# Second layer's mixture of experts: ways up as three products of 16-bit halves, computed two experts ahead

## The chip, the cores and the metric

One core of one Trainium2 chip. The metric is device time in microseconds (us) of one launch, the median of several runs. The core has a matmul engine (PE, with its weight loads PEld), a vector engine (DVE), an activation engine (ACT), GpSimd (POOL) and a queue engine (SP) that issues the DMAs. They run side by side and are ordered by semaphores only.

## The reference, cut to what matters

The model has four layers, each an attention over a context of 8 x 1500 rows followed by a feed-forward part, on 8 x 56 = 448 tokens of width 128. The change touches the feed-forward part of the second layer, a mixture of experts:

```
logits = x @ router_w.T                      # 16 experts, the best 2 of each token
w_full = sigmoid(top 2 logits), else 0
h      = silu(x @ gate_e) * (x @ up_e)       # each expert: 128 -> 128, twice
moe    = sum_e w_full[e] * (h @ down_e)
shared = silu(x @ sg) * (x @ su) @ sd        # width 256
x      = x + tanh(g_ffn[1]) * (moe + shared)
```

Here x is the normalised token matrix. All 16 experts are computed for all tokens and weighted afterwards; the shared part of width 256 is cut into two more "experts" of weight 1, which makes 18 in all.

## The kernel before, in words

The program is one hand-written instruction stream for each engine. The order within a stream is that of the code; between engines it is set by counting semaphores (`wait_ge` on one engine, `then_inc` on another).

The stage of the second layer's experts runs from about 322 to 367 us of the span. Names of its steps:

- The weights come in groups of three experts (`G1 = 3`, six groups). One DMA of 576 KB brings a group: for each expert 128 columns of gate, of up and of down, in 32-bit floats, into one of two buffers `wex[0]`, `wex[1]` (line 612). Groups 0 and 1 are loaded long before; group g + 2 is issued when group g's last product down is done (`ex_dn`).
- `gate_up1` (lines 1081 to 1088), called GU(e) from here on: PE computes gate and up of expert e, two products of 128x128 weights by 128x448 tokens, both operands 32-bit. Each such product shows as two MATMUL records in the trace, so GU(e) is four. Its two results go to PSUM banks 2, 3 or 4, 5 in turn.
- `silu1` (line 1564): ACT takes silu of the gate bank.
- `hidden1` (line 2332, recorded as line 1898 since all two-operand vector operations pass one helper): DVE multiplies it by the up bank; h goes to `xT2` or `xT3`.
- The product down (line 1099), called D(e): PE computes four products of 128x112 hidden values by 128x128 weights, both 32-bit, eight records in the trace, into bank 6 or 7.
- `weigh` (also recorded as line 1898): DVE multiplies the result of D(e) by the token's weight for e.
- `add_expert` (line 1798): POOL adds that to the running sum `y2`.

PE's order is GU(0), then for each e: GU(e + 1), D(e). GU(e + 1) waits for the hidden values of expert e - 1, whose banks it takes. D(e) waits for the hidden values of e and for the weighing of e - 2. DVE's order is hidden(e + 1), weigh(e). Both are written as hardware loops of two or six experts. Ahead of the loop DVE also works out the router's choice: two calls of `pick`, some 15 small instructions, between hidden(0) and weigh(0). ACT takes the router's sigmoid after silu(1).

Ahead of the stage stand the second layer's attention (lines 1010 to 1050 on PE; `probs1` and copies on ACT; `shift1` and `normalise1` on DVE), the output projection, the residual, a layer norm and four transposes, which give `xT`. Behind it DVE adds the sum and the last two experts' results to x (line 1942), and a layer norm leads on to the third layer's attention.

The fourth layer's experts (from about 753 us) already use three products of 16-bit halves: ACT rounds the 32-bit weights to 16 bits (`split_hi3`, line 1665: the high half), DVE subtracts that from the original (`split_lo3`, line 2548: the low half), the tokens are split alike, and PE sums high x high, high x low and low x high in one PSUM bank (line 1334).

Of the kernel before, what the change touches and what calls it, by code (L numbers as in the profile page):

```python
# [8 lines left out]
F16 = mybir.dt.float16  # L9
BF16 = mybir.dt.bfloat16  # L10
U8 = mybir.dt.uint8
ALU = mybir.AluOpType
# [101 lines left out]
SETS = 4  # L114
SQ = 6
G1 = 3

CTX_TOP, LATE_AT, SQK_AT = 19370, 23466, 29346

# [11 lines left out]

PRODUCT = {"latent_q": 14, "latent_k": 18, "latent_qT": 19, "queries2": 23, "queries3T": 36}

MAX_BANKS, TURN = (4, 5, 7), 24
MAX_AHEAD = 32
MAX_ORDER = [(0, u) for u in range(24)]
# [65 lines left out]
def build(nc, io, out):  # L202
    ctx = ExitStack()
    with ctx:
# [155 lines left out]
        w_r1 = carve([D, 16])  # L360
        sm16 = carve([TT, 8, NT, 16])
        wts = carve([TT, NT, E1])
        l1_end = at[0]
        ktmp = arena[:, ktmp_at:ktmp_at + B * D].rearrange("p (b n) -> p b n", b=B)
        at[0] = core_end
# [170 lines left out]
        def _(sp):  # L536
# [90 lines left out]
            for u in range(16, 24):  # L627
                if u == 19:
                    sp.wait_ge(rn_sq, 1)
                    for v in range(20, 24):  # L630
                        load_later(v)
                store_later(u)
                if u == 16:
                    sp.wait_ge(lv_full, 16 - IN_TURNS + 1)
                    load_experts1(0, 0)
                if u == 19:
                    sp.wait_ge(lv_full, 19 - IN_TURNS + 1)
                    load_experts1(1, 1)
# [5 lines left out]
            with sp.Fori(0, E1 // G1 // 2 - 1) as i:  # L644
                for p in range(2):
                    g = 2 * i + p
                    sp.wait_ge(ex_dn, G1 * (g + 1))
                    load_experts1(g + 2, p)


            sp.wait_ge(lat_ready, 1)
# [76 lines left out]
                load_gate_up3(e, e)  # L728
                load_down3(e, e)
            for e in range(E3 - 2):  # L730
                sp.wait_ge(ex_split, e + 1)
# [16 lines left out]
        def _(pe):  # L748
# [325 lines left out]
            op.next()  # L1074
            by_tokens(xT, w_r1, 1, cols=16)

            def w1(k, group, col):

                return wex[group][:, D * (3 * k + col):D * (3 * k + col) + D]

            def gate_up1(s, loads):

                if s % G1 == 0:
                    pe.wait_ge(ex_ld[s // G1 % 2], 16 * loads)
# [5 lines left out]
            def expert1(turn, s, more=True):  # L1090
                e = 2 * G1 * turn + s
                if more:

                    pe.wait_ge(ex_h, e + 1)
                    gate_up1(s + 1, turn + 1 + (s + 1) // (2 * G1))
                pe.wait_ge(ex_w, e + 1)
                pe.wait_ge(ex_h, e + 2)
                for t in range(NT):
                    mm = pe.matmul(ps[0:TT, 6 + s % 2, D * t:D * t + D],
                                   (xT2, xT3)[s % 2][:, TT * t:TT * t + TT], w1(s % G1, s // G1 % 2, 2),  # L1100
                                   start=True, stop=True)
                mm.then_inc(ex_dn, 1)

            gate_up1(0, 1)
            pe.wait_ge(lk_taken, 24 - IN_TURNS)
            pe.wait_ge(lv_taken, 24 - IN_TURNS)
            with pe.Fori(0, E1 // (2 * G1) - 1) as i:
                for s in range(2 * G1):
                    expert1(i, s)
            for s in range(2 * G1):  # L1110
                expert1(E1 // (2 * G1) - 1, s, more=s < 2 * G1 - 1)


            pe.wait_ge(ld_m, 5 * 16)
# [235 lines left out]
                mm.then_inc(ex_dn, 1)  # L1350

            def expert3(e, p):
                pe.wait_ge(ex_split, e + 1)
# [26 lines left out]
        def _(act):  # L1380
# [160 lines left out]
            later(20)  # L1541
            probs1(0)
            later(21)
            for i in range(NT):
                if i + 1 < NT:
# [12 lines left out]


            later(23)  # L1560

            def silu1(e, p):
                act.wait_ge(ex_gu, e + 1)
                act.activation(exs[p], ps[0:D, 2 + 2 * p, 0:N], ACT.Silu).then_inc(ex_act, 1)  # L1564

            silu1(0, 0)
            silu1(1, 1)
            act.wait_ge(to_act, 1)
            act.activation(sm16[:, 6], sm16[:, 0], ACT.Sigmoid).then_inc(from_act, 1)
            with act.Fori(1, E1 // 2) as i:  # L1570
                for p in range(2):
                    silu1(2 * i + p, p)


            act.wait_ge(l2_m, 1)
# [89 lines left out]
                act.copy(wh3[p][:, 0, :], wex[p][:, 0:2 * FF]).then_inc(ex_hi, 1)  # L1665

            def down_hi3(e, p):
                act.wait_ge(ex_ldd[p], 16 * (e // 2 + 1))
# [223 lines left out]
        def _(dve):  # L1892
# [4 lines left out]
            def tt(out, a, b, op):  # L1897
                return dve.tensor_tensor(out, a, b, op)  # L1898
# [397 lines left out]
            for i in range(NT):  # L2296
                if i + 2 < NT:
                    shift1(i + 2)
                if i == 2:

                    dve.wait_ge(rn_sd, 1)
                    ch.step(dve.reciprocal(rn_flat, rn_flat))
                normalise1(i)
            product_in.next()
            ch.link(tt(y, ps[0:TT, 0, :].rearrange("p (t n) -> p t n", t=NT), spread("L1_ob"), ALU.add))
            residual(1, y)
# [17 lines left out]
            layernorm(x, z, 1e-5)  # L2324
            signal(operand)
            turned(xT, 0)
            product_in.next()
            dve.tensor_copy(sm16[:, 0], ps[0:TT, 1, 0:64].rearrange("p (t n) -> p t n", t=NT)).then_inc(to_act, 1)

            def hidden1(e, p):  # L2330
                dve.wait_ge(ex_act, e + 1)
                tt((xT2, xT3)[p], ps[0:D, 3 + 2 * p, 0:N], exs[p], ALU.mult).then_inc(ex_h, 1)

            def weigh(e, p, weight, first):

# [11 lines left out]
                residual(k, big[:, :, D:2 * D])  # L2347
                dve.nop().then_inc(ex_acc, 1)

            hidden1(0, 0)  # L2350
            dve.wait_ge(to_act, 1)
            pick(sm16, 16, 0, NEG)
            hidden1(1, 1)
# [6 lines left out]
            weigh(0, 0, wts[:, :, 0:1], 0)  # L2360
            hidden1(2, 0)
            weigh(1, 1, wts[:, :, 1:2], 0)
            with dve.Fori(1, E1 // 2 - 1) as i:
                for p in range(2):
                    e = 2 * i + p
                    hidden1(e + 1, 1 - p)
                    weigh(e, p, wts[:, :, bass.ds(e, 1)], 0)
            hidden1(E1 - 1, 1)
            dve.wait_ge(ex_acc, E1)
            residual(5, y2)  # L2370
            for e in range(E1 - 2, E1):
# [172 lines left out]

            def split_lo3(e, p):

                dve.wait_ge(ex_hi, e + 1)
# [144 lines left out]
```

## Time and profile before

| what | value |
|---|---|
| median of 3 runs | 826.67 us (825.04 to 827.05) |
| the profiled execution's own time | 825.94 us |
| its span | 824.1 us |
| PE busy | 735.4 us (89%) |
| DVE busy | 615.2 us (75%) |
| ACT busy | 438.3 us (53%) |
| POOL busy | 347.0 us (42%) |
| mean granted TensorE clock | 0.943 of full |

The span is measured from the first to the last instruction; 1.8 us of the profiled execution's time lie around it. Busy shares are averages over stages with different limits, so the stage of the change has to be read by itself.

### The profile page before, as it was taken

The page shows a single profiled execution, that of the slowest core. Times are in us where ns is not written, and L with a number is a line of the kernel's source. Part 1 is how long each engine was busy: PE and PEld are TensorE (multiplying, and loading weights), DVE is VectorE, ACT ScalarE, POOL GpSimd, SP SyncE. Part 2 cuts the span into 40 slices and gives each one's busy share as a digit, 9 for nine tenths or more (in the row PEclk, how much of TensorE's full clock was granted, in tenths as well). Part 3 has the DMA queues.
Part 4 walks back from the last instruction along what each step waited for, and adds up shares of the span by engine and source line. Part 5 has one row for each costly group of instructions (what it writes and reads, how often), then busy time and mean ns, then how long its engine had stood idle before and what let it go on. Part 6 is the DMA issues. An engine that isn't in the chain of part 4 may idle for free.

```text
span 824.1 us, 15426 instructions
## 1 busy us (share of the span) xinstructions
PE 735.4 (89%) x5468; PEld 469.1 (57%) x5468; DVE 615.2 (75%) x1297; ACT 438.3 (53%) x739; POOL 347.0 (42%) x283
## 2 busy tenths in 40 slices
PE   3799999997886978998899999998899999898997
PEld 3577787776544465663455555563346666653443
DVE  4779999998878765567565566658689999516786
ACT  2656667677484433435444545432127776743674
POOL 0665555561523501640677787740242211102464
PEclk8999999999998878999999999999859999999999
DMA  8267767532424512206022333007736678101520
GB/s 208 75 205 252 252 198 227 173 117 72 98 67 131 160 51 76 86 29 177 3 79 78 104 100 101 6 10 103 128 71 131 124 126 165 37 2 64 180 78 12
DMA packets 50645, 89.71 MB, mean 109 GB/s; under 512 B 17427, under 2 KB 34779, under 8 KB 50099
## 3 DMA queue, kind: packets, MB, share of 16 engines
q1 hardware_dynamic: 50578, 88.83, 39.8%
q8 instruction: 42, 0.69, 0.4%
q14 instruction: 25, 0.20, 0.1%
HBM read 63.29 MB, written 25.52 MB: 108 GB/s over the span
## 4 chain that ended last, share of the span: by engine, by line
PE 29%; DVE 17%; POOL 2%; ACT 2%; issue 2%; DVEq 0%; POOLq 0%; ACTq 0%
DVE arena L2516 11%; PE ps L1165 9%; PE ps L1155 7%; PE ps L1334 3%; PE ps L1348 2%; DVE arena L1898 2%; POOL arena L1820 2%; PE ps L1270 2%; PE ps L1259 1%; ACT arena L1647 1%; PE ps L1201 1%; PE ps L1242 1%; PE ps L1313 1%; PE ps L1171 1%; PE ps L768 1%
## 5 line engine op out<-in xcount | busy, mean ns | idle before, releaser
L2516 DVE TENSOR_REDUCE arena<-ps 112x1 f32<-112x500 f32 x192 | 114.6, 670 | 9.0 <-PE ps L1242 9.0
L1820 POOL TENSOR_TENSOR arena<-arena 125x448 f32<-125x448 f32 x96 | 109.2, 1137 | 24.6 <-ACT arena L1606 20.7
L1898 DVE TENSOR_TENSOR arena<-ps,arena 128x448 f32<-128x448 f32 (+7 forms) x139 | 80.8, 612 | 37.5 <-ACT arena L1564 18.3
L1647 ACT ACTIVATE arena<-ps 125x896 f32<-125x896 f32 x96 | 87.2, 917 | 23.5 <-PE ps L1259 23.4
L1165 PE MATMUL ps<-arena 125*128 125x448 f32 (+1 forms) x208 | 97.2, 548 | 2.0 <-ACT arena L1606 1.5
L1606 ACT ACTIVATE arena<-arena,kbias 125x448 f32<-125x448 f32 x96 | 63.6, 668 | 65.4 <-DVE arena L1898 47.9
L1898 DVE TENSOR_TENSOR arena<-ps,rn 125x448 f32<-125x448 f32 x96 | 59.2, 618 | 47.0 <-PE ps L1155 42.1
L843 PE MATMUL ps<-w_k2h,arena 128*125 128x512 f16 x288 | 69.4, 392 | 11.6 <-ACT arena L1416 10.4
L1155 PE MATMUL ps<-arena 128*125 128x448 f16 (+3 forms) x312 | 76.5, 354 | 1.2 <-DVEq L1909 1.1
L1155 PEld LDWEIGHTS ps<-arena 128*125 128x125 f16 (+1 forms) x312 | 40.1, 133 | 54.8 <-issue 41.8
L1416 ACT ACTIVATE arena<-ps 125x512 f32<-125x512 f32 x96 | 55.4, 598 | 12.4 <-PE ps L843 9.8
L843 PEld LDWEIGHTS ps<-w_k2h,arena 128*125 128x125 f16 x288 | 39.2, 140 | 36.5 <-ACT arena L1416 14.5
L2052 DVE TENSOR_REDUCE rn<-arena 125x8 f32<-125x512 f32 x96 | 59.0, 679 | 0.8 <-ACT arena L1416 0.8
L1242 PE MATMUL ps<-arena 64*112 64x500 f16 x192 | 55.4, 444 | 2.5 <-issue 1.2
L1732 POOL TENSOR_TENSOR arena<-arena 128x500 f16<-128x500 f32 x24 | 27.4, 1144 | 69.4 <-ACT arena L1403 69.2
L1270 PE MATMUL ps<-arena 125*32 125x168 f32 x768 | 48.6, 325 | 2.3 <-ACT arena L1647 1.8
L1898 DVE TENSOR_TENSOR arena<-arena 125x12 f32<-125x12 f32 (+6 forms) x79 | 45.9, 597 | 6.2 <-ACT arena L1681 4.7
L866 PE MATMUL ps<-w_l,arena 128*125 128x256 f32 x192 | 44.7, 390 | 1.8 <-ACT arena L1443 1.8
L1165 PEld LDWEIGHTS ps<-arena 125*128 125x128 f32 (+1 forms) x208 | 37.7, 189 | 14.6 <-issue 8.8
L1334 PE MATMUL ps<-arena 128*128 128x448 f16 x192 | 40.9, 361 | 5.5 <-DVE arena L1898 5.5
L1716 POOL TENSOR_TENSOR arena<-arena 112x4 f32<-112x4 f32 x9 | 9.2, 1027 | 83.6 <-DVE arena L1922 75.1
L1259 PE MATMUL ps<-arena 64*125 64x112 f16 x768 | 43.5, 235 | 0.0
(323 smaller groups left out, 1462.7 us busy)
## 6 DMA issues: line engine op xcount, KB each, us to landing
arena<-in_ctxT SPq DMA_DIRECT2D x8, 750.0 KB, 9.3
d_cln<-arena SPq DMA_DIRECT2D x8, 750.0 KB
d_clnT<-arena SPq DMA_DIRECT2D x8, 750.0 KB
d_k<-arena SPq DMA_DIRECT2D x24, 250.0 KB
d_v<-arena SPq DMA_DIRECT2D x24, 250.0 KB
arena<-d_clnT SPq DMA_DIRECT2D x8, 750.0 KB
arena<-in_ctx SPq DMA_DIRECT2D x8, 672.0 KB
arena<-d_cln SPq DMA_DIRECT2D x8, 672.0 KB
```

Source lines behind the costliest of these rows:

```text
L843: mm = pe.matmul(ps[0:KP, k, :], clnT[p][:, a, KP * j:KP * j + KP], w_k2h[:, w, :], start=(n == 0), stop=(n == 2))
L1155: mm = pe.matmul(ps[0:rows, (t + p) % 2, 0:N].rearrange("p (h q) -> p h q", h=H8), clnT_s[p][:, a, cols:cols + rows], qtT[:, q, :, bass.ds ...
L1165: pe.matmul(ps[0:D, 4 + 2 * p, 0:N], cln_s[p][0:rows, t, :], pexp[(t + p) % 2][0:rows], start=(t == 0), stop=(t == KT)).then_inc(l2_pv, 1)
L1242: pe.matmul(ps[0:TT, max_bank(bn, u), 0:500], q.rearrange("p o h q -> p (o h q)"), kst[bn % 3][64 * r:64 * r + 64, g, 500 * third:500 * th ...
L1270: pe.matmul(ps[32 * g:32 * g + 32, 6, 0:168], v3s[p][:, t, 32 * g:32 * g + 32], p3[t % 2][:, 3 * g:3 * g + 3, :].rearrange("p h q -> p (h ...
L1334: mm = pe.matmul(ps[0:D, 2 + 2 * (c % 2) + m, 0:N], wh3[p][:, w, at:at + D], xTh[:, a, :], start=(n == 0), stop=(n == 2))
L1606: act.activation(pexp[(t + p) % 2][0:rows], sscl[(t + p) % 2][0:rows], ACT.Exp, bias=bias)\
L1647: act.activation(p3[t % 2].rearrange("p (k h) q -> p k (h q)", k=2), ps[0:KP, 2 * (t % 2):2 * (t % 2) + 2, 0:8 * S], ACT.Exp).then_inc(l3_ ...
L1820: ins = pool.tensor_tensor(psum2[p][0:rows], psum2[p][0:rows], pexp[(t + p) % 2][0:rows], ALU.add)
L1898: return dve.tensor_tensor(out, a, b, op)
L2052: dve.tensor_reduce(rn[:, bass.ds(turn - 1, 1), j, :].rearrange("p o h -> p (o h)"), sqk[:, j % SQ, :].rearrange("p (h d) -> p h d", h=H8) ...
L2516: dve.tensor_reduce(mx3[bn % 2][:, u % 2, u % 8 // 2, u // 8:u // 8 + 1], ps[0:TT, max_bank_of(bn, u), 0:500], AX.X, ALU.max).then_inc(l3_ ...
```

## The change

- GU(e) becomes six 16-bit products in place of two 32-bit ones: high x high, high weights x low tokens, low weights x high tokens, for gate and for up. Banks come in three pairs, (2, 3), (4, 5), (0, 1), and the hidden values and silu results in three buffers.
- PE's order becomes GU(0), GU(1), then for each e: GU(e + 2), D(e). GU(e) waits for the halves of its group (`ex_split`) and for hidden(e - 3).
- New on ACT: `split_hi1(g)`, the rounding of a group's 768 columns of gate and up; groups 0 and 1 in the attention, ahead of `probs1(3)`; groups 2 to 5 after silu(3), silu(6), silu(9) and silu(12). Also the rounding of `xT`.
- New on DVE: `split_lo1(g)`, the subtraction; groups 0 and 1 after the last `normalise1`, groups 2 to 5 after hidden(3), hidden(6), hidden(9) and hidden(12). Also the low half of `xT`, between the copy that makes `xT` and the copy of the router's logits.
- DVE's order becomes weigh(e), hidden(e + 2).
- The group's load is two DMAs: gate and up (384 KB), issued as soon as the halves of the group before it in the same buffer are made; down (192 KB), issued after that group's last D. The halves and third buffers lie in `kblk`, which the attention has left.
- The loops are written out. The fourth layer's waits on the shared counters are moved by what is counted here.

```diff
-            def load_experts1(g, p):
-                sp.dma_start(wex[p][:, 0:G1 * 3 * D], batch(io["L1_ex"], g)).then_inc(ex_ld[p], 16)
+            def load_gate_up1(g, p):
+                sp.dma_start(wex[p][:, 0:GU1], io["L1_ex"][g, :, 0:GU1]).then_inc(ex_ld[p], 16)
+            def load_down1(g, p):
+                sp.dma_start(wex[p][:, GU1:G1 * 3 * D], io["L1_ex"][g, :, GU1:G1 * 3 * D]).then_inc(ex_ldd[p], 16)
...
+            sp.wait_ge(ex_split, 2)
+            for p in range(2):
+                load_gate_up1(2 + p, p)
+            for g in range(E1 // G1 - 2):
+                sp.wait_ge(ex_dn, G1 * (g + 1))
+                load_down1(g + 2, g % 2)
+                if g + 4 < E1 // G1:
+                    sp.wait_ge(ex_split, g + 4)
+                    load_gate_up1(g + 4, g % 2)
...
+            def gate_up1(e):
+                g, at = e // G1, e % G1 * 2 * D
+                pe.wait_ge(ex_split, 3 if g < 2 else g + 2)
+                if e > 2:
+                    pe.wait_ge(ex_h, e - 1)
                 for m in range(2):
-                    mm = pe.matmul(ps[0:D, 2 + 2 * (s % 2) + m, 0:N], w1(s % G1, s // G1 % 2, m), xT,
-                                   start=True, stop=True)
+                    for n, (w, a) in enumerate(((0, 0), (0, 1), (1, 0))):
+                        mm = pe.matmul(ps[0:D, UP_BANKS1[e % 3] - 1 + m, 0:N], wh1[g % 2][:, w, at + D * m:at + D * m + D],
+                                       x1h[:, a, :], start=(n == 0), stop=(n == 2))
...
+            gate_up1(0)
             pe.wait_ge(lk_taken, 24 - IN_TURNS)
             pe.wait_ge(lv_taken, 24 - IN_TURNS)
+            gate_up1(1)
+            pe.wait_ge(to_act, 1)
+            for e in range(E1):
+                if e + 2 < E1:
+                    gate_up1(e + 2)
+                down1(e)
...
+            def split_hi1(g):
+                act.wait_ge(ex_ld[g % 2], 16 * (g // 2 + 1))
+                if g > 1:
+                    act.wait_ge(ex_gu, G1 * (g - 1))
+                act.copy(wh1[g % 2][:, 0, :], wex[g % 2][:, 0:GU1]).then_inc(ex_hi, 1)
...
+            act.wait_ge(operand, OPERAND["latentsT"] - 2)
+            act.copy(x1h[:, 0, :], xT).then_inc(ex_hi, 1)
...
+            def split_lo1(g):
+                dve.wait_ge(ex_hi, g + 1 if g < 2 else g + 2)
+                tt(wh1[g % 2][:, 1, :], wex[g % 2][:, 0:GU1], wh1[g % 2][:, 0, :], ALU.subtract).then_inc(ex_split, 1)
...
+            for e in range(E1 - 2):
+                weigh(e, e % 2, wts[:, :, e:e + 1], 0)
+                hidden1(e + 2)
+                if e % G1 == 1 and e // G1 + 2 < E1 // G1:
+                    split_lo1(e // G1 + 2)
```

## Rows read from the trace of the kernel before

**Rows 1.** Busy time by stretch, the stage: from:to us, length, engines, clock, DMA.
```profile
322.00:366.30 44.30, 43.58 (x218) 29.14 (x217) 24.98 (x51) 21.60 (x28) 20.28 (x16) 1.00 0.22 75
```

**Rows 2.** Timeline of the stage: start us, us, engine, line, operation, [idle before <- releaser].
```profile
359.66 1.28 ACT L1564 ACT_TABLE_LOAD   x1
359.77 1.67 PE L1086 MATMUL ps<-arena,wex 128*128 128x448 f32 x4
361.04 1.27 POOL L1798 TENSOR_TENSOR arena<-arena 112x512 f32<-112x512 f32 x1 [1.11 <-DVE arena L1898]
361.27 1.04 PE L1099 MATMUL ps<-wex,arena 128*112 128x128 f32 x8
...
362.05 1.22 DVE L1898 TENSOR_TENSOR arena<-ps,arena 128x448 f32<-128x448 f32 x2 [1.16 <-ACT arena L1564]
362.15 1.67 PE L1086 MATMUL ps<-arena,wex 128*128 128x448 f32 x4
```

**Rows 3.** The chain that ended last: start us, us, what.
```profile
398.20 0.75 PE ps L1165 x2
398.96 0.57 PE ps L1155 x3
...
789.80 2.27 PE ps L1348 x12
```

**Rows 4.** Timeline of the stage's start.
```profile
321.99 3.25 PE L1086 MATMUL ps<-arena,wex 128*128 128x448 f32 x8
...
323.78 0.54 ACT L1564 ACTIVATE arena<-ps 128x448 f32<-128x448 f32 x1 [4.88 <-PE ps L1086]
...
328.98 2.35 DVE L1898 TENSOR_TENSOR arena<-ps,arena 112x512 f32<-112x512 f32 x4
...
330.25 1.13 PE L1099 MATMUL ps<-wex,arena 128*112 128x128 f32 x8 [0.21 <-DVE arena L1898]
...
331.53 0.69 DVE L1898 TENSOR_TENSOR arena<-ps,arena 112x512 f32<-112x512 f32 x1 [0.20 <-PE ps L1099]
```

**Rows 5.** Timeline of the fourth layer's experts, which work with halves.
```profile
752.11 1.22 DVE L1898 TENSOR_TENSOR arena<-wex,arena 128x1024 f16<-128x1024 f32 x1
...
753.46 2.43 PE L1334 MATMUL ps<-arena 128*128 128x448 f16 x12
...
754.79 0.54 ACT L1675 ACTIVATE arena<-ps 128x448 f32<-128x448 f32 x1 [0.31 <-PE ps L1334]
755.24 1.04 ACT L1665 CAST arena<-wex 128x1024 f16<-128x1024 f32 x1
...
761.23 0.56 ACT L1681 CAST arena<-arena 128x448 f16<-128x448 f32 x1 [2.38 <-DVE arena L1898]
...
761.83 0.63 DVE L1898 TENSOR_TENSOR arena<-arena 128x448 f16<-128x448 f32 x1 [0.63 <-ACT arena L1681]
...
777.60 1.34 DVE L1898 TENSOR_TENSOR arena<-arena 128x448 f16<-128x448 f32 x1 [0.69 <-ACT arena L1681]
```

**Rows 6.** Timeline of the second layer's attention and what follows it.
```profile
298.04 1.06 ACT L1539 ACTIVATE arena<-arena 128x1024 f32<-128x1024 f32 x1 [3.93 <-DVE arena L1898]
...
313.65 0.69 DVE L1898 TENSOR_TENSOR arena<-ps,vec 112x512 f32<-112x512 f32 x1 [2.96 <-PE ps L760]
```

**Rows 7.** Timeline of the DMA queue, and the landing of line 612's loads.
```profile
320.26 0.52 SPq L642 DMA_DIRECT2D arena<-in_L_wq  x1
...
DMA to landing us min/median/max: 3.5/3.7/7.8
```

**Rows 8.** Timeline of the stage's end.
```profile
366.75 0.75 DVE L1942 SCALAR_TENSOR_TENSOR x<-ps,tg,x 112x512 f32<-112x512 f32 x1 [0.25 <-DVE x L1942]
```

**Rows 9.** Busy time by stretch, around the stage (columns as in rows 1).
```profile
300.00:310.00 10.00, 7.97 (x37) 7.41 (x35) 5.63 (x7) 1.57 (x4) 0.00 (x0) 0.50 0.01 2
368.00:372.00 4.00, 4.00 (x24) 2.07 (x21) 3.52 (x17) 1.02 (x1) 1.06 (x1) 0.57 0.00 0
384.00:388.00 4.00, 2.98 (x8) 1.52 (x10) 2.27 (x5) 1.20 (x3) 0.00 (x0) 0.64 1.06 268
```

More of the change, by code:

```diff
@@ L116 @@
 G1 = 3
+GU1 = G1 * 2 * 128
+SPLITS1 = 7
 CTX_TOP, LATE_AT, SQK_AT = 19370, 23466, 29346
@@ L132 @@
 PRODUCT = {"latent_q": 14, "latent_k": 18, "latent_qT": 19, "queries2": 23, "queries3T": 36}
+UP_BANKS1 = (3, 5, 1)
 MAX_BANKS, TURN = (4, 5, 7), 24
@@ L362, in build @@
         wts = carve([TT, NT, E1])
+        wh1, h1, ex1 = [], [xT2, xT3], [exs[0], exs[1]]
+        for p in range(2):
+            words = kblk[p].rearrange("p e h s -> p (e h s)")
+            wh1.append(words[:, 0:768].bitcast(F16).rearrange("p (w n) -> p w n", w=2))
+            (h1, ex1)[p].append(words[:, 768:768 + N])
+        x1h = kblk[0].rearrange("p e h s -> p (e h s)")[:, 768 + N:768 + 2 * N].bitcast(F16).rearrange("p (w n) -> p w n", w=2)
         l1_end = at[0]
@@ L634, in _ @@
                     sp.wait_ge(lv_full, 16 - IN_TURNS + 1)
-                    load_experts1(0, 0)
+                    load_gate_up1(0, 0)
+                    load_down1(0, 0)
                 if u == 19:
                     sp.wait_ge(lv_full, 19 - IN_TURNS + 1)
-                    load_experts1(1, 1)
+                    load_gate_up1(1, 1)
+                    load_down1(1, 1)
             sp.wait_ge(lv_full, 23 - IN_TURNS + 1)
@@ L642, in _ @@
                 sp.dma_start(dst, io[name]).then_inc(ld_m, 16)
[L644 to L648, printed above, removed]
+            sp.wait_ge(ex_split, 2)
+            for p in range(2):
+                load_gate_up1(2 + p, p)
[5 more added lines that the diff above has]
+                    load_gate_up1(g + 4, g % 2)
             sp.wait_ge(lat_ready, 1)
@@ L730, in _ @@
             for e in range(E3 - 2):
-                sp.wait_ge(ex_split, e + 1)
+                sp.wait_ge(ex_split, SPLITS1 + e + 1)
                 load_gate_up3(e + 2, e % 2)
@@ L1075, in _ @@
             by_tokens(xT, w_r1, 1, cols=16)
[L1077 to L1084, printed above, removed]
+            def gate_up1(e):
[3 more added lines that the diff above has]
+                    pe.wait_ge(ex_h, e - 1)
@@ L1085, in gate_up1, with down1 @@
                 for m in range(2):
-                    mm = pe.matmul(ps[0:D, 2 + 2 * (s % 2) + m, 0:N], w1(s % G1, s // G1 % 2, m), xT,
-                                   start=True, stop=True)
+                    for n, (w, a) in enumerate(((0, 0), (0, 1), (1, 0))):
+                        mm = pe.matmul(ps[0:D, UP_BANKS1[e % 3] - 1 + m, 0:N], wh1[g % 2][:, w, at + D * m:at + D * m + D],
+                                       x1h[:, a, :], start=(n == 0), stop=(n == 2))
                 mm.then_inc(ex_gu, 1)
[L1090 to L1095, printed above, removed]
+            def down1(e):
+                g = e // G1
+                if e % G1 == 0:
+                    pe.wait_ge(ex_ldd[g % 2], 16 * (g // 2 + 1))
@@ L1096, in expert1 @@
                 pe.wait_ge(ex_w, e + 1)
                 pe.wait_ge(ex_h, e + 2)
+                at = GU1 + e % G1 * D
                 for t in range(NT):
-                    mm = pe.matmul(ps[0:TT, 6 + s % 2, D * t:D * t + D],
-                                   (xT2, xT3)[s % 2][:, TT * t:TT * t + TT], w1(s % G1, s // G1 % 2, 2),
-                                   start=True, stop=True)
+                    mm = pe.matmul(ps[0:TT, 6 + e % 2, D * t:D * t + D], h1[e % 3][:, TT * t:TT * t + TT],
+                                   wex[g % 2][:, at:at + D], start=True, stop=True)
@@ L1102, in expert1 @@
                 mm.then_inc(ex_dn, 1)
-            gate_up1(0, 1)
+            gate_up1(0)
             pe.wait_ge(lk_taken, 24 - IN_TURNS)
             pe.wait_ge(lv_taken, 24 - IN_TURNS)
[L1107 to L1111, printed above, removed]
+            gate_up1(1)
[4 more added lines that the diff above has]
+                down1(e)
@@ L1352, in expert3 @@
             def expert3(e, p):
-                pe.wait_ge(ex_split, e + 1)
+                pe.wait_ge(ex_split, SPLITS1 + e + 1)
                 for c in range(4):
@@ L1543, in _ @@
             later(21)
+            def split_hi1(g):
[3 more added lines that the diff above has]
+                act.copy(wh1[g % 2][:, 0, :], wex[g % 2][:, 0:GU1]).then_inc(ex_hi, 1)
             for i in range(NT):
+                if i == NT - 2:
+                    act.wait_ge(l1_s, NT)
+                    split_hi1(0)
+                    split_hi1(1)
                 if i + 1 < NT:
@@ L1560, in _, with silu1 @@
             later(23)
-            def silu1(e, p):
+            act.wait_ge(operand, OPERAND["latentsT"] - 2)
+            act.copy(x1h[:, 0, :], xT).then_inc(ex_hi, 1)
+            def silu1(e):
                 act.wait_ge(ex_gu, e + 1)
[L1564 to L1572, printed above, removed]
+                act.activation(ex1[e % 3], ps[0:D, UP_BANKS1[e % 3] - 1, 0:N], ACT.Silu).then_inc(ex_act, 1)
+            for e in range(E1):
+                silu1(e)
+                if e == 1:
+                    act.wait_ge(to_act, 1)
+                    act.activation(sm16[:, 6], sm16[:, 0], ACT.Sigmoid).then_inc(from_act, 1)
+                if e % G1 == 0 and 1 < e // G1 + 1 < E1 // G1:
+                    split_hi1(e // G1 + 1)
             act.wait_ge(l2_m, 1)
@@ L2303, in _ @@
                 normalise1(i)
+            def split_lo1(g):
+                dve.wait_ge(ex_hi, g + 1 if g < 2 else g + 2)
+                tt(wh1[g % 2][:, 1, :], wex[g % 2][:, 0:GU1], wh1[g % 2][:, 0, :], ALU.subtract).then_inc(ex_split, 1)
+            split_lo1(0)
+            split_lo1(1)
             product_in.next()
@@ L2326, in _, with hidden1 @@
             turned(xT, 0)
+            dve.wait_ge(ex_hi, 3)
+            dve.wait_ge(operand, OPERAND["latentsT"] - 2)
+            tt(x1h[:, 1, :], xT, x1h[:, 0, :], ALU.subtract).then_inc(ex_split, 1)
             product_in.next()
             dve.tensor_copy(sm16[:, 0], ps[0:TT, 1, 0:64].rearrange("p (t n) -> p t n", t=NT)).then_inc(to_act, 1)
-            def hidden1(e, p):
+            def hidden1(e):
                 dve.wait_ge(ex_act, e + 1)
-                tt((xT2, xT3)[p], ps[0:D, 3 + 2 * p, 0:N], exs[p], ALU.mult).then_inc(ex_h, 1)
+                tt(h1[e % 3], ps[0:D, UP_BANKS1[e % 3], 0:N], ex1[e % 3], ALU.mult).then_inc(ex_h, 1)
             def weigh(e, p, weight, first):
@@ L2348, in weigh_last @@
                 dve.nop().then_inc(ex_acc, 1)
-            hidden1(0, 0)
+            hidden1(0)
             dve.wait_ge(to_act, 1)
             pick(sm16, 16, 0, NEG)
-            hidden1(1, 1)
+            hidden1(1)
             pick(sm16, 16, 1, NEG)
@@ L2358, in _ @@
             ch.link(dve.memset(wts[:, :, 16:E1], 1.0))
[L2360 to L2368, printed above, removed]
+            for e in range(E1 - 2):
[3 more added lines that the diff above has]
+                    split_lo1(e // G1 + 2)
             dve.wait_ge(ex_acc, E1)
@@ L2639 @@
                                a["L1_ffn_shared_down_w"][:, D * k:D * k + D].T], axis=1) for k in range(2)]
+    all1 = np.concatenate([experts1, np.stack(shared1)]).reshape(-1, G1, D, 3 * D)
     io = {
```

8 lines of the change are left out of this document (4 added, 4 removed).

## The prediction

> **What bounds the kernel now.** I read the page first, but its shares are averages over stages, so next the view of busy time by stretch for the stage of the second layer's experts. [...] PE bounds the stage. The timeline gives its period: GU(16) starts at 359.77, D(15) at 361.27, GU(17) at 362.15 [rows 2]. So GU takes a slot of 1.50 us, D one of 0.88, an expert 2.38. The other engines wait inside it: DVE sat idle 1.16 us for the silu, POOL 1.11 us for DVE [rows 2]. Behind the stage the token path goes on without a branch (residual, layer norm, projections, the third attention), so what the stage's end gains, the whole gains.
>
> **PE's slots.** GU goes from two 32-bit products to six 16-bit ones of the same 448 columns. The fourth layer has such products back to back: 12 in 2.27 us, 0.189 each [rows 3]. Six make 1.135 in place of 1.50. D keeps its 32 bits and its 0.88. Does a change of type between them cost something? In the third layer three 16-bit products and one 32-bit product alternate, 398.20 + 0.75 = 398.95 and the next begins at 398.96 [rows 3]; nothing. New period 1.135 + 0.88 = 2.02 us, 0.365 less. [...] I take 0.365, from back-to-back work.
>
> **Does the chain of hand-overs fit into 2.02?** D(e)'s start to weigh(e)'s start is 331.53 - 330.25 = 1.28 us [rows 4]. DVE's pair of weigh and hidden takes 1.22 [rows 2], the hand-over to PE about 0.15 (an estimate: the four vector operations end at 328.98 + 2.35 = 331.33, of which the second, hidden(2), at about 330.15; D(2) starts at 330.25 [rows 4]). So D(e) to D(e + 2) needs 1.28 + 1.22 + 0.15 = 2.65, and has 4.04. On the other side GU's start to silu takes 754.79 - 753.46 = 1.33 [rows 5], so GU(e + 2)'s silu is done 1.33 + 0.54 = 1.87 after its start, and D(e + 2) follows 5.2 us after it. Looking two experts ahead leaves both loops slack of over a microsecond. PE stays the bound.
>
> **DVE's new work in the stage.** The low half of 768 columns lies between 448 columns at 0.63 and 1024 at 1.22 [rows 5], 0.95 in proportion. Three experts cost 3 x 1.22 + 0.95 = 4.6 of 6.05 us. One instruction can be stretched: the subtraction at 777.60 took 1.34 in place of 0.63 with GpSimd at work beside it [rows 5], 0.7 more. With it DVE has 5.3 of 6.05; still covered. If the cover were gone (over 1.4 us more for each of the four halves), the excess would be paid four times.
>
> [...]
>
> **ACT.** A silu is 0.54; four roundings of 768 columns lie between 0.56 and 1.04 [rows 5], 0.8 each. ACT has 3 x 0.54 + 0.8 = 2.4 of 6.05 us. The loops reload a table before every other silu, 1.28 us, which lies in ACT's wait for PE [rows 2]; the unrolled form drops seven of nine or so. That was hidden, so it earns nothing.
>
> **The start.** Halves of groups 0 and 1: ACT's 2 x 0.8 go ahead of probs1(3), where ACT waited 3.93 us for DVE [rows 6]; DVE's 2 x 0.95 go into the 2.96 us that it waited for the projection [rows 6]. Their loads were issued by 278 and land within 7.8 [rows 7]. Cost nothing; if that cover failed, up to 1.6 + 1.9. The token halves lie on the path: after `xT` ACT rounds (0.56), DVE subtracts (0.63) [rows 5], and then PE may begin; the router's eight products fill part of it, and GU(0) starts about 322.45 in place of 321.99. But what ends last is DVE's chain: silu(0), hidden(0), the router's small instructions, weigh(0), hidden(2), then D(2) at 330.25, where PE had waited [rows 4]. silu(0) comes 1.33 after GU's start with 16 bits and came 323.78 - 321.99 = 1.79 after it [rows 4], so silu(0) moves from 323.78 to 323.8. D(2) stays at 330.25 to 330.4: I take +0.1. The gain of the first experts' shorter GU thus goes into PE's wait there. Bounds: 0 to +0.5.
>
> **From D(2) on.** After D(2) come 13 periods to D(15) in both orders (a GU and a D each): 13 x 0.365 = 4.75. In the trace D(15) starts at 361.27, and (361.27 - 330.25) / 13 = 2.386, so no stall hides in between.
>
> **The tail.** D(15), weigh(15), POOL's add, three residuals. GU(17) no longer stands between D(15) and D(16), but the third residual does not wait for them: it runs right behind the second (idle 0.25) [rows 8], and all three behind POOL. Before, DVE did hidden(16) between D(15) and weigh(15), late by 0.05; now weigh comes at once. D(17) waits for hidden(17), behind weigh(15): 1.28 + 1.22 + 0.15 = 2.65 after D(15), and its result is there before the third residual. D(15)'s start to the end stays 367.50 - 361.27 = 6.2. Change 0, bounds -0.1 and +0.3.
>
> **Loads.** Twelve DMAs for six; four more issues of some 0.5 us [rows 7] beside an idle SP. Gate and up of groups 2 and 3 are now issued right behind the third layer's weights (320.26 and on [rows 7]); even at the longest landing of 7.8 [rows 7] they are there by 329.6, and split_hi1(2) is due at about 329.8, its halves at 334. Down of group g + 2 has three D's of time, 6 us, against 3.7. SP's two new waits stand ahead of nothing but these loads until the latents' store, 5 us after the stage. Counters of the fourth layer are only renumbered.
>
> **Sum.** 4.75 - 0.1 = 4.6 us. The profiled execution took 825.94, so 821.3; it lies 0.7 below the median of 826.67, against which later medians are to be held: 822.1.
>
> **The rivals.**
> 1. The period doesn't fall to 2.02, because hand-overs and waits on PE's queue (two or three before each group of products) leave gaps. For it: PEld shows idle "issue" gaps everywhere. Against: they lie under running products. At 0.15 a period more, 2 us of the gain go: 824.1; at the full 0.365 nothing is left: 826.7. I give 0.10, around 824.6.
> 2. More than forecast: DVE's chain at the start ends earlier, since ACT and PE are less in its way, and D(2) comes up to 1 us sooner, or a dip of the clock behind the stage goes away. In 384 to 388 us the granted clock was 0.64, in 368 to 372 it was 0.57 [rows 9], with keep-up products and critical ones in them. 820.0; 0.08.
> 3. [...] 823.6; 0.06.
> 4. Slower than before: the clock falls in the stage. PE now has a wait before GU(0) and one before D(2); from 300 to 310 us, where it was busy 8.0 of 10 us, the grant was 0.50 [rows 9]. [...] Against it: PE is 98% busy in the stage of before [rows 1], both new waits are under half a microsecond, and the fourth layer's halves run at 0.189 each, the full clock, in a stage with waits too [rows 3]. 0.05.
>
> The rest, 0.71, is the forecast with its own range of 820.6 to 823.6.
>
> **How the numbers follow.** Likeliest 822.0. 820.2 to 824.6 takes in the slot's bounds (1.21: 1.0 later), the start's, the clock both ways and part of the first rival. What this measurement can tell from no change is about 0.3%, 2.5 us: faster is below 824.2, slower above 829.1. Faster: 0.71 + 0.08 + 0.06 and a little of the first rival, 0.86; same 0.09; slower 0.05.
>
> **What would show it.** In the changed trace GU as six records with the next D 1.14 behind it; a period of 2.02 from D(2) to D(15); D(2) at 330.3; DVE idle in each period, split_lo1 at 0.95 to 1.7; the third residual's end at 362.9 in place of 367.5; the same distance from there to the end. A period above 2.1, a D(2) after 331, a clock below 1.00 in the stage, or a part behind the stage that grew would make it wrong.

## The result, and the profile after

The changed kernel takes 822.12 us (median of 20 runs, 816.84 to 829.01) beside 827.14 us for the kernel before (20 runs, 822.48 to 830.12): ratio 0.9952, 95% interval 0.9931 to 0.9973. In absolute terms that is 4.0 us less by the ratio (2.2 to 5.7) and 5.0 by the medians. Forecast were 822.0 us and 4.6 less. That the median lies within 0.1 us of the forecast is luck: runs of one kernel spread over more than 1%, and the parts below miss by more. So the parts of the forecast are read from the profiles, where the same stretch repeats to a few hundredths of a microsecond.

Three marks cut the kernel into parts: the start of DVE's copy that makes the transposed tokens (from there the stage is measured, its length called T), the end of the third residual, and the first product of the third layer's attention. From the page of the changed kernel:

```profile
span 818.4 us, 15421 instructions
```

| part, us | before | changed | difference |
|---|---|---|---|
| up to the transposed tokens | 320.50 | 322.08 | +1.58 |
| T, the stage | 47.00 | 41.66 | -5.34 |
| of it: tokens to D(2) | 9.75 | 9.68 | -0.07 |
| of it: D(2) to D(15), 13 periods | 31.02 | 26.22 | -4.80 |
| of it: D(15) to the third residual's end | 6.23 | 5.76 | -0.47 |
| from there to the third layer's first product | 25.35 | 24.17 | -1.18 |
| the rest of the span | 431.25 | 430.49 | -0.76 |
| span | 824.1 | 818.4 | -5.7 |

The stage was profiled a second time in both kernels: T 47.00 again before, 41.65 changed. The first and the last part vary from profile to profile of any kernel here (317.0 to 322.1 and 430.5 to 436.2). So the change's own effect is the 5.35 of the stage; the first profiles' 5.7 holds other things that nearly cancel. The part behind the stage repeated in each kernel (25.35 and 25.34 before, 24.17 twice in the changed one). Its busy rows (from:to us, length, PE, PEld, DVE, ACT, POOL, granted clock, DMA share, GB/s), before and changed, show where the difference comes from, a mean granted clock of 0.87 and 1.00:

```profile
367.50:392.85 25.35, 21.42 (x85) 10.10 (x85) 20.01 (x48) 11.77 (x22) 1.06 (x1) 0.87 0.56 145
363.74:387.91 24.17, 18.20 (x84) 8.52 (x85) 19.91 (x48) 11.52 (x22) 1.06 (x1) 1.00 0.59 152
```

The 1.58 us more ahead of the tokens do not come from the new halves of groups 0 and 1. These lie wholly in waits. First the kernel before, then the changed one:

```profile
311.57 2.05 PE L760 MATMUL ps<-arena 128*112 128x128 f32 x8 [0.34 <-ACT arena L1532]
```
```profile
299.08 1.06 ACT L1555 ACTIVATE arena<-arena 128x1024 f32<-128x1024 f32 x1 [2.46 <-DVE arena L1926]
...
312.30 1.83 DVE L1926 TENSOR_TENSOR arena<-wex,arena 128x768 f16<-128x768 f32 x2
313.15 2.05 PE L778 MATMUL ps<-arena 128*112 128x128 f32 x8 [0.34 <-ACT arena L1548]
...
315.23 0.69 DVE L1926 TENSOR_TENSOR arena<-ps,vec 112x512 f32<-112x512 f32 x1 [1.10 <-PE ps L778]
```

ACT's wait fell from 3.93 us to 2.46 and DVE's from 2.96 to 1.10 ([rows 6] has both of before), and from the projection's first product to the tokens it is 320.50 - 311.57 = 8.93 before and 322.08 - 313.15 = 8.93 after.

Busy time over the whole of T, in the same columns, first the kernel before between the same two marks, since [rows 1] covers a shorter stretch, then the changed one. PE's waits now lie at the two ends, and DVE's share has risen by the new halves, from 57% to 78%:

```profile
320.50:367.50 47.00, 45.02 (x227) 30.05 (x225) 26.56 (x53) 21.60 (x28) 20.28 (x16) 1.00 0.23 77
322.08:363.74 41.66, 38.41 (x263) 28.17 (x261) 32.61 (x58) 17.25 (x27) 21.21 (x16) 1.00 0.27 86
```

The timeline of one period with a split (start us, us, engine, line, operation, idle before), beside [rows 2]. GU is now six records of 16 bits; GU(10) starts at 342.75, D(8) at 343.89, 1.14 later, and the next GU at 344.76; 344.76 - 342.75 is the period, 2.01:

```profile
342.52 0.82 ACT L1564 CAST arena<-wex 128x768 f16<-128x768 f32 x1
...
342.75 1.30 PE L1103 MATMUL ps<-arena 128*128 128x448 f16 x6
342.95 1.22 DVE L1926 TENSOR_TENSOR arena<-ps,arena 112x512 f32<-112x512 f32 x2 [0.79 <-PE ps L1115]
...
343.79 1.27 POOL L1826 TENSOR_TENSOR arena<-arena 112x512 f32<-112x512 f32 x1 [0.58 <-DVE arena L1926]
343.89 1.03 PE L1115 MATMUL ps<-wex,arena 128*112 128x128 f32 x8
...
344.09 1.78 DVE L1926 TENSOR_TENSOR arena<-wex,arena 128x768 f16<-128x768 f32 x1
...
344.76 1.30 PE L1103 MATMUL ps<-arena 128*128 128x448 f16 x6
```

The subtraction took 1.78 us: POOL's add had begun at 343.79 and ended at 345.06, and the subtraction ended at 345.87, 0.81 later. In all four groups: 0.95, 1.78, 1.78, 1.78. In the first it was the add that took longer, 2.14 in place of 1.27 (332.61 to 334.75), although its record starts 0.05 before the subtraction's.

The stage's start, beside [rows 4]: D(2) at 331.76 is 9.68 us behind the tokens; weigh(0) starts at 330.39, hidden(2) follows it, and PE still waits for that:

```profile
322.08 0.62 DVE L1976 COPY arena<-ps 128x448 f32<-128x448 f32 x1 [0.79 <-PE ps L772]
...
322.74 0.56 ACT L1588 CAST arena<-arena 128x448 f16<-128x448 f32 x1 [3.63 <-DVE arena L1976]
...
324.02 3.59 PE L1103 MATMUL ps<-arena 128*128 128x448 f16 x18 [0.30 <-DVE arena L1926]
325.37 0.55 ACT L1592 ACTIVATE arena<-ps 128x448 f32<-128x448 f32 x1 [0.76 <-PE ps L1103]
...
330.39 2.35 DVE L1926 TENSOR_TENSOR arena<-ps,arena 112x512 f32<-112x512 f32 x4
...
331.73 0.93 PEld L1115 LDWEIGHTS ps<-wex,arena 128*112 128x112 f32 x8 [0.54 <-issue]
331.76 1.10 PE L1115 MATMUL ps<-wex,arena 128*112 128x128 f32 x8
```

The stage's end, beside [rows 8]. DVE waits 0.91 for POOL's last add, and the three residuals follow:

```profile
357.98 1.91 PE L1115 MATMUL ps<-wex,arena 128*112 128x128 f32 x16
...
359.05 1.22 DVE L1926 TENSOR_TENSOR arena<-ps,arena 112x512 f32<-112x512 f32 x2 [0.79 <-PE ps L1115]
359.88 1.26 POOL L1826 TENSOR_TENSOR arena<-arena 112x512 f32<-112x512 f32 x1 [0.74 <-DVE arena L1926]
...
361.19 0.75 DVE L1970 SCALAR_TENSOR_TENSOR x<-arena,tg,x 112x512 f32<-112x512 f32 x1 [0.91 <-POOL arena L1826]
361.97 0.75 DVE L1970 SCALAR_TENSOR_TENSOR x<-ps,tg,x 112x512 f32<-112x512 f32 x1
362.99 0.75 DVE L1970 SCALAR_TENSOR_TENSOR x<-ps,tg,x 112x512 f32<-112x512 f32 x1 [0.26 <-DVE x L1970]
```

### The profile page after: what moved, and what is told of

Same layout as the page of the kernel before. It is cut to its first block, busy times and chain, and to the rows that moved or that the text cites. A ratio compares the mean times of both kernels' runs of the same rounds, so it can differ in the third digit from the quotient of the medians.

```text
span 818.4 us, 15421 instructions
## 1 busy us (share of the span) xinstructions
PE 727.2 (89%) x5504; PEld 467.2 (57%) x5504; DVE 623.2 (76%) x1304; ACT 434.1 (53%) x739; POOL 348.1 (43%) x283
## 4 chain that ended last, share of the span: by engine, by line
PE 30%; DVE 16%; ACT 3%; POOL 2%; issue 2%; DVEq 0%; POOLq 0%; ACTq 0%
DVE arena L2550 10%; PE ps L1181 9%; PE ps L1171 6%; PE ps L1350 3%; PE ps L1286 2%; PE ps L1364 2%; DVE arena L1926 2%; PE ps L1275 2%; POOL arena L1848 2%; PE ps L1258 1%; ACT arena L1675 1%; PE ps L1217 1%; PE ps L1329 1%; PE ps L1187 1%; PE ps L786 1%
## 5 line engine op out<-in xcount | busy, mean ns | idle before, releaser
L1926 DVE TENSOR_TENSOR arena<-arena 125x12 f32<-125x12 f32 (+7 forms) x80 | 46.5, 598 | 6.8 <-ACT arena L1709 4.7
L1874 POOL COPY arena<-arena 4x448 f16<-4x448 f16 x16 | 8.9, 554 | 80.4 <-ACT arena L1661 79.9
```

## The experiments

Parts of T in every profile, in us. A dip is a stretch, 3.4 us long or twice that, in which the granted clock is at its lower level, 0.50 of the full one (337.93 to 341.34 of the version with one load, for example); the last column says whether one lay at the stage's start.

| kernel | tokens to D(2) | 13 periods | tail | T | behind the stage | clock's dip at the start |
|---|---|---|---|---|---|---|
| before, two profiles | 9.75 | 31.02 | 6.23 | 47.00 | 25.35, 25.34 | no |
| changed, two profiles | 9.68, 9.67 | 26.22 | 5.76 | 41.66, 41.65 | 24.17 | no |
| 32-bit products, order of the change, two | 12.53 | 30.93 | 5.76 | 49.22 | 25.39, 25.40 | yes |
| one ahead, 16 bits | 9.67 | 26.22 | 6.00 | 41.89 | 24.17 | no |
| two products | 9.30 | 21.30 | 5.76 | 36.36 | 25.39 | no |
| two products, no low halves | 9.29 | 21.30 | 5.76 | 36.35 | 25.28 | no |
| subtractions twice | 9.67 | 28.73 | 5.76 | 44.16 | 25.21 | no |
| one load for a group | 10.91 | 48.89 | 5.76 | 65.56 | 24.97 | yes |
| other tail | 11.06 | 26.15 | 4.87 | 42.08 | 25.32 | yes |
| other tail, PE kept busy | 9.68 | 26.22 | 4.87 | 40.77 | 25.67 | no |
| one choice of the router | 10.95 | 26.15 | 5.76 | 42.86 | 25.80 | yes |

**32-bit products in the change's order.** Everything of the change but the halves:

```diff
-                    for n, (w, a) in enumerate(((0, 0), (0, 1), (1, 0))):
-                        mm = pe.matmul(..., wh1[g % 2][:, w, at + D * m:at + D * m + D],
-                                       x1h[:, a, :], start=(n == 0), stop=(n == 2))
+                    mm = pe.matmul(..., wex[g % 2][:, at + D * m:at + D * m + D], xT, start=True, stop=True)
...
+                sp.wait_ge(ex_gu, G1 * (g + 1))
+                load_gate_up1(g + 2, g % 2)
```

> The changed kernel's order (two experts ahead), three bank pairs, three buffers, written-out loops, and loads of ways up and down apart, but products of 32-bit operands and no halves at all. Stage T = from the start of the copy that makes the transposed tokens to the end of the third residual; 47.0 us in the kernel before, 41.7 in the changed one. Theory A (PE's slots set the period; only the shorter products pay): period 2.38 to 2.39 us from D(2) to D(15), T 46.3 to 47.0 (only the tail, where weigh(15) no longer stands behind hidden(16), gives 0.3 to 0.5), whole kernel within 1 us of before. Rival B (the order, the loads apart or the written-out loops carry a good part): period under 2.25, T below 45, whole kernel 2 us or more faster than before.

The period stayed at 30.93 / 13 = 2.38 us and the tail gave its 0.47: theory A, for these two parts. T was 49.22, outside both theories, and the whole kernel slower than before, ratio 1.0033 (1.0007 to 1.0058). The loss stands at the start, where D(2) came 2.8 us later: three GUs took 6.45 us.

> The kernel with 32-bit products, two ahead, once more. Its first profile had T 49.2, of which 2.8 were a dip of the clock at the start, and its time was 3 us over before. Theory: the dip comes and goes, so T is 46.4 in a profile without it, 49.2 with it, and the period 2.38 in both. Rival: this order always has the dip or another cost, T 49.2 again.

It was 49.22 again (ratio 1.0023, 1.0000 to 1.0045). The rows of the second profile, first PE's timeline, then the granted clock:

```profile
322.57 6.45 PE L1099 MATMUL ps<-arena,wex 128*128 128x448 f32 x12
328.86 1.04 PE L1111 MATMUL ps<-wex,arena 128*112 128x128 f32 x8
...
332.12 1.67 PE L1099 MATMUL ps<-arena,wex 128*128 128x448 f32 x4
333.62 1.04 PE L1111 MATMUL ps<-wex,arena 128*112 128x128 f32 x8
```
```profile
322.00:326.00 4.00, 4.00 (x13) 2.20 (x13) 0.23 (x1) 0.32 (x1) 0.00 (x0) 0.61 0.66 232
```

Twelve records at the full clock are 12 x 0.375 = 4.5 us; here D(0) starts 328.86 - 322.57 = 6.29 us after GU(0), since for 3.4 us the clock was at its lower level, where a record took 0.75 us in place of 0.375. So the dip is 1.8 of the 2.8 us; the expectation above, and below that of the version with PE kept busy, put all 2.8 down to it, which is wrong. The other 1.0 is the order's own: ahead of D(2) PE now has five GUs and two D's in place of four and two. From the tokens that is 1.48 + 5 x 1.50 + 2 x 0.88 = 10.74 us even without a dip, where DVE's chain needed 9.75 before. With 16-bit GUs the same five fit under the chain (9.68). Without the dip T would be about 47.4 (an estimate, 49.22 - 1.8), not 46.4. The rival "a dip or another cost" stands: two profiles of two show 49.22, and the whole times agree (1.8 + 1.0 - 0.6 for periods and tail = 2.2 us or 0.27%).

**One expert ahead.**

```diff
-                if e + 2 < E1:
-                    gate_up1(e + 2)
+                if e + 1 < E1:
+                    gate_up1(e + 1)
                 down1(e)
```

> The changed kernel with its 16-bit products, but only one expert ahead as before: PE GU(e+1), D(e); DVE hidden(e+1), weigh(e); the low half of a group made after weigh(2), weigh(5), weigh(8), weigh(11). Theory A (slots set the period; a hand-over GU to D takes 2.67 us and has 3.15): period 2.02 to 2.1, at most some 0.2 us lost at each of the four split places, T 41.9 to 43.0. Rival B (the look-ahead carries the gain): T 45 to 47.

T 41.89, at the lower end of theory A, with the full 26.22 of the changed kernel. Looking two experts ahead buys nothing for the period; all that is lost is 0.24 of the tail, since hidden(16) stands ahead of weigh(15) again. Time 823.85 us, ratio 0.9969 (0.9944 to 0.9995). Two rows show what the later place of the split does:

```profile
343.31 0.95 DVE L1925 TENSOR_TENSOR arena<-wex,arena 128x768 f16<-128x768 f32 x1
...
343.54 1.85 POOL L1825 TENSOR_TENSOR arena<-arena 112x512 f32<-112x512 f32 x1 [0.74 <-DVE arena L1925]
```

Here DVE began first, took its 0.95, and POOL's add was the one that stretched, to 1.85.

**Two products.** `enumerate(((0, 0), (0, 1)))` in place of the three; then also without the subtraction:

```diff
+                if g < 2:
                     tt(wh1[g % 2][:, 1, :], wex[g % 2][:, 0:GU1], wh1[g % 2][:, 0, :], ALU.subtract).then_inc(ex_split, 1)
+                else:
+                    dve.nop().then_inc(ex_split, 1)
```

> The changed kernel without the third product of each way up (low weights by high tokens left out), halves made as before. PE's slots shrink from 2.02 to 1.64 us. Theory A alone: period 1.64, T 36.8. Theory C (DVE is the next bound, because the four subtractions were stretched to 1.78 us beside GpSimd: 3 x 1.22 + 1.78 = 5.4 us for three experts): period 1.80 to 1.85 over the groups with a split, T 38.5 to 39.5.

> As the one with two products (the third left out), and DVE's low halves of groups 2 to 5 left out too (a nop signals in their place). Theories A and C: DVE and GpSimd have 1.22 and 1.27 us of 1.64, so period 1.64 to 1.66, T 36.6 to 37.2. If hand-overs bound instead (D(e) to D(e+2) 2.5 us against 3.28), period above 1.7.

Both periods are 21.30 / 13 = 1.64 us: PE's slots again, and theory C fell. T is 36.36 and 36.35, a little under what was expected, since D(2) came sooner too. The subtractions took 0.95 in all four groups with two products: three began within 0.06 us of the start of POOL's add, the second 0.12 before the end of one (333.09, the add's end at 333.21), and POOL's adds beside them took 1.9 to 2.1. I had carried 1.78 over to another rhythm. The first two of them:

```profile
328.42 0.95 DVE L1926 TENSOR_TENSOR arena<-wex,arena 128x768 f16<-128x768 f32 x1
333.09 0.95 DVE L1926 TENSOR_TENSOR arena<-wex,arena 128x768 f16<-128x768 f32 x1
```

One more reading: D(2) came 0.37 us sooner, as GU(0) is 0.38 shorter, though PE's work ahead of D(2) shrank by 5 x 0.38 = 1.9. So a chain from silu(0) over DVE sets D(2), not PE's sum.

**Each subtraction twice.**

```diff
+                if g > 1:
+                    ch.link(tt(wh1[g % 2][:, 1, :], wex[g % 2][:, 0:GU1], wh1[g % 2][:, 0, :], ALU.subtract))
```

> The changed kernel with each of DVE's four subtractions in the stage made twice over. Theory A with C (DVE covered, but only just: 3 x 1.22 + 1.78 = 5.4 of 6.05 us): now about 6.4 of 6.05, so PE waits some 0.3 to 0.6 us for each group, T 42.3 to 43.8. If the halves were on the path already, each copy would cost its whole 0.95 to 1.8: T 45.5 to 48. If DVE had ample room: T 41.7.

T 44.16, a little over the range: 2.5 us more, of which 1.05 in the first group and 0.49 in each of the other three. A group now takes 6.53 us (341.61 to 348.13 below), set by DVE: two subtractions 2.97 and three pairs.

```profile
341.61 2.97 DVE L1926 TENSOR_TENSOR arena<-wex,arena 128x768 f16<-128x768 f32 x2
344.50 2.34 DVE L1926 TENSOR_TENSOR arena<-ps,arena 112x512 f32<-112x512 f32 x4
346.99 1.22 DVE L1926 TENSOR_TENSOR arena<-ps,arena 112x512 f32<-112x512 f32 x2 [0.15 <-PE ps L1115]
```

So the halves are covered in the changed kernel: in those three groups DVE had 1.2 us more, of which 0.5 reached the end and 0.7 was room; in the first it had 1.9 more (2.89 for 0.95), of which 0.9 was room.

**One load for a group**, as before, after its last D:

```diff
-                load_down1(g + 2, g % 2)
-                if g + 4 < E1 // G1:
-                    sp.wait_ge(ex_split, g + 4)
-                    load_gate_up1(g + 4, g % 2)
+                load_group1(g + 2, g % 2)
```

> The changed kernel with one DMA of 576 KB for a group of three experts, issued after the group's last product down, as in the kernel before; all else as changed. Theory: ACT's rounding of group g stands behind silu(3g-3) and then waits for a load issued only after D(3g-4), 3.7 us long, and the silu behind it waits with it; some 2.8 us for each of four groups, T 50 to 54, slower than before by 3 to 7 us. Rival (the separate loads are of no consequence, since the old load had time enough): T 41.7.

Time 846.48 us, ratio 1.0222 (1.0172 to 1.0273); T 65.56, far over my 50 to 54. The direction was right and the size less than half: 24 us more than the changed kernel, where 8 to 12 were expected. The timeline shows the ring (PE, ACT and SP):

```profile
331.18 11.86 SPq L621 DMA_DIRECT2D wex<-in_L_ex  x2
...
334.80 0.83 ACT L1561 CAST arena<-wex 128x768 f16<-128x768 f32 x1 [5.24 <-DMA wex<-in_L_ex]
...
336.68 1.31 PE L1100 MATMUL ps<-arena 128*128 128x448 f16 x6 [3.51 <-DVE arena L1923]
...
339.69 2.12 PE L1100 MATMUL ps<-arena 128*128 128x448 f16 x6
...
346.77 0.83 ACT L1561 CAST arena<-wex 128x768 f16<-128x768 f32 x1 [8.20 <-DMA wex<-in_L_ex]
```

A group took 346.77 - 334.80 = 11.97 us in place of 6.05. The load of a group waits for three D's that come only after the silus queued behind the rounding of the group ahead, so load, rounding, silu and three experts follow one another instead of overlapping; and behind a wait of PE of 3.5 us the granted clock was at 0.50 from 337.93 to 341.34 (2.12 us for six products). The change's loads "apart" are what makes halves possible at this place of ACT's queue; another place for the rounding was not tried.

**Other tail.** Expert 16's residual ahead of the wait for POOL:

```diff
-            dve.wait_ge(ex_acc, E1)
-            residual(5, y2)
             for e in range(E1 - 2, E1):
+                if e == E1 - 1:
+                    dve.wait_ge(ex_acc, E1)
+                    residual(5, y2)
```

> The changed kernel as it is, on the same chip as the one with the other tail. T 41.5 to 41.8, whole kernel 0.4 to 0.7% under before. The part from the stage's end to the third layer's first product was 24.2 us in its first profile and 25.4 before; theory: that is the clock's dips, so it varies from run to run between about 24 and 25.5 whatever the kernel.

T was 41.65 as expected, the time 0.59% under before. The part behind the stage was 24.17 once more, so its theory, that this part varies from run to run whatever the kernel, is not borne out: all three kernels with two profiles repeated their own value (the last is 25.39 and 25.40 of the 32-bit version).

> The changed kernel with the three last residuals in another order: expert 16's result is added to x while GpSimd still makes the last sum, then the sum, then expert 17. Theory A: the tail from D(15) to the last residual is a chain weigh(15), GpSimd's add 1.27, three residuals of 0.75; one residual moves into DVE's wait of 0.91 for GpSimd, T 40.7 to 41.0, whole kernel 0.8 us less than the changed one (too little for its time to show). Rival: expert 16's result is late and the order gains nothing, T 41.6.

The tail fell from 5.76 to 4.87 as worked out, DVE's wait for POOL from 0.91 to 0.26:

```profile
356.41 0.74 DVE L1970 SCALAR_TENSOR_TENSOR x<-ps,tg,x 112x512 f32<-112x512 f32 x1
357.40 0.75 DVE L1970 SCALAR_TENSOR_TENSOR x<-arena,tg,x 112x512 f32<-112x512 f32 x1 [0.26 <-POOL arena L1826]
358.31 0.75 DVE L1970 SCALAR_TENSOR_TENSOR x<-ps,tg,x 112x512 f32<-112x512 f32 x1 [0.15 <-DVE x L1970]
```

T itself was 42.08, since this profile had the dip at the start (+1.39). Of the complete versions this has the lowest median: 820.67 us, ratio to before 0.9911 (0.9883 to 0.9939), beside 822.10 and 0.9941 (0.9913 to 0.9970) of the changed kernel on the same chip. The intervals overlap; that it beats the kernel before is shown, that it beats the changed one only by the profile's 0.89.

**PE kept busy around the stage.** The other tail, and more keep-up products (`keep_clock`: products that nobody reads, run while PE would wait): 11 in place of 6 ahead of the token transposes, 10 new ones behind D(17), 11 in place of 7 ahead of the latents' transposes.

> The changed kernel with the tail's new order and more keep-up products on TensorE where it waits around the stage: 11 in place of 6 ahead of the token transposes, 10 new ones behind D(17), 11 in place of 7 ahead of the latents' transposes. In the profiles so far the clock was at its lower level for about 3.5 us either right behind the start of the stage (T + 1.4 with 16-bit products, + 2.8 with 32-bit ones) or at two places behind it (25.3 in place of 24.2 us from the stage's end to the third layer's first product). Theory F (the dips follow the waits just ahead of them, where PE was busy 0.65 of 2 us): start and end of the stage stay at 1.00, T 40.7 to 40.9, the part behind 24.2 to 24.8 (the dip before the query products isn't filled), whole kernel 0.6 to 1.0% under before. Rival (the dips come whatever PE does there): one of them in this profile too.

No dip at the start nor right behind the stage, T 40.77, as theory F said. The changed kernel's two profiles have none at either place without the filling, so this one profile doesn't show that the filling kept them away. And ahead of the third layer the clock was low for 6.8 us and soon after for another 3.4, and the part behind rose to 25.67; time 823.19, ratio 0.9958 (0.9935 to 0.9981), no better than the changed kernel:

```profile
320.00:325.00 5.00, 4.80 (x29) 2.99 (x30) 2.91 (x12) 3.59 (x6) 0.00 (x0) 1.00 0.82 303
359.03:363.00 3.97, 3.97 (x30) 2.16 (x29) 3.29 (x17) 1.01 (x1) 1.06 (x1) 1.00 0.00 0
376.00:380.00 4.00, 3.44 (x10) 1.82 (x12) 2.24 (x5) 1.25 (x4) 0.00 (x0) 0.50 1.07 260
```

**One choice of the router** (`pick(sm16, 16, 1, NEG)` left out, a product of the first choice with itself in its place, so the second expert of each token is missing from the result).

> The changed kernel with the router's second choice left out (a single small product in its place, so some 1.5 us less in DVE's chain ahead of weigh(0)). Theory (DVE's chain sets D(2), PE waits 0.3 to 0.5 us for it): D(2) 9.3 to 9.4 us after the transposed tokens in place of 9.67, no more, because PE's own slots set it then; T 41.3. Rival (D(2) was set by PE or by the halves): 9.67, T 41.65.

Inconclusive: this profile had the dip, and D(2) at 10.95 says no more than the 11.06 and 10.91 of the two other 16-bit versions with one. The two products above speak for DVE's chain instead.

**The kernel before, a second profile.**

> The kernel before as it is, a second profile. Its first had no dip of the clock at the stage's start (T 47.0) and two behind it (25.4 to the third layer's first product). The kernel with 32-bit products two ahead had the dip at the start in both of its profiles. [...]

T 47.00 and 25.34 behind: no dip at the start and two behind the stage, as in the first profile. Why this kernel has none at the start and the 32-bit version of the new order has one each time, it doesn't tell.

## Why the prediction was right

- PE bounds, and the period falls from 2.38 to 2.02: measured 26.22 / 13 = 2.017. Shown by taking it apart: 32-bit products in the new order keep 2.38, 16-bit ones in the old order reach 2.02, two products give 1.64. Rival 1 (gaps in the hand-overs) is out. The 13 periods gave 4.80 for 4.75. The stage as a whole gave 5.34 where the sum had 4.65: 0.05 more from the periods, 0.17 from the start and 0.47 from the tail. The 1.21 us for a GU in the forecast's range is half the 2.43 of [rows 5]; no run shows such a slot: six records took 1.14 (342.75 to D(8) at 343.89); only their modelled end is at 1.30.
- D(2) stays where it was: 9.75 became 9.68, forecast +0.1. silu(0) came 1.35 us after GU(0)'s start, as [rows 5] had it at 1.33. The halves of groups 0 and 1 cost nothing, as forecast: 8.93 us from the projection to the tokens in both kernels.
- The tail was the term mis-sized: forecast 0 (bounds -0.1 and +0.3), measured -0.47, beyond its bounds. I had seen that hidden(16) no longer stands ahead of weigh(15) but took 1.28 from D to weigh from [rows 4]; that row is not of the steady rhythm: its D had waited 0.21 for DVE, its weights were loaded only then, and its record is 1.13 long where the steady ones are 1.03. In the steady rhythm it is 342.95 - 341.88 = 1.07. The same step missed that hidden(17) stood ahead of the first residual before: POOL's add ended at 364.69 and DVE was free for the residual at 364.97.
- Splits: ACT 0.82 each, DVE 0.95 to 1.78 (forecast 0.95 to 1.7), all covered, as doubling them showed. Where POOL had begun first, by 0.3 us, the subtraction ended 0.81 us after POOL's add, and with DVE first it was POOL that took longer (1.85 for 1.27). The 0.83 more lie near my 0.7 from [rows 5], and DVE had room for them: 3 x 1.22 + 1.78 = 5.4 of 6.05 us.
- Loads: in time; gate and up took 3.5 to 7.8 us to land, down 2.3 to 7.6, so none more than the forecast's longest, and no rounding in the stage waited for one. What I did not weigh was what they would cost if not apart: 24 us.
- The clock: rival 2 spoke of the dips of [rows 9]. In both profiles of the changed kernel they were gone (24.17 for 25.35), which is rival 2's condition, yet the time did not come out at its 820.0. Of the variants, all but the one that looks one ahead show at least one of them. So 1.2 us of the first profile's gain come from the clock and not from the stage. They repeated in the second pair of profiles, but the whole time leaves little room for them: 5.35 + 1.2 = 6.5 lies above its interval of 2.2 to 5.7. No run here ties them to the edit.

Open: why the dip at the start came in both profiles with 32-bit products two ahead, in neither of the kernel before, and in some with 16 bits.

## What to carry to other kernels

Where TensorE's slots bound a loop, write down the slot of each product from back-to-back records at hand, and the longest hand-over beside it; if the hand-over fits with room, the saving is the slots' and deeper look-ahead is worth nothing for the period (26.22 us for 13 of them here, one expert ahead or two). It can cost at the start of the loop, where it puts one more product group ahead of the first consumers: 1.0 us with 32-bit products here, nothing with 16-bit ones. Then ask of each new producer (here the rounding and its load) what stands behind it in its queue: a load that lands ahead of its reader cost nothing here (those of the changed kernel), one that closes a ring can cost about a group's whole time (6 us for each of four groups here). Take the distance from a product to its reader from the steady rhythm, not from a place where the product itself had waited. And before a loss is put down to a dip of the clock, work out what the dip can cost: at a granted clock of 0.50 products took twice their time, which cost about half of the dip's length here, 1.8 of 3.4 us.

## What the runs showed of the hardware

- A 16-bit product of 448 columns takes 0.19 us and a 32-bit one 0.75, and alternating six 16-bit products with D's 32-bit ones cost nothing here: 1.14 + 0.88 = 2.02, and 13 periods took 26.22, 2.017 each.
- DVE's subtraction and POOL's add take longer beside each other: the subtraction 1.78 us for 0.95 when POOL had begun 0.3 us before, the add 1.85 for 1.27 when DVE had begun 0.23 before. With 0.06 us or less between the two starts, the add was the longer one (2.07 to 2.14).
- In and behind the stage the granted clock fell to 0.50 of the full one at up to three places, for 3.4 us at a time (6.8 once in the profiles with PE kept busy, with one choice and with one load); the version with one load has more of them. The changed kernel and the one that looks one ahead have none. At the stage's start it cost 1.2 to 1.4 us with 16-bit products and 1.8 with 32-bit ones. The wait just ahead does not settle it: in the last 2 us before the tokens PE was busy 0.64 to 0.65 us in all profiles but the filled one, with the dip and without.
